# A cross-attention, state-space and expert block on one core: six of sixteen states added by DMA instead of TensorE, and token numbers scattered instead of rows

## The reference

```
x = x + cross_attention(norm(x), ctx)      # 8 heads, softmax(q k^T / 8) v, projections with bias
x = x + selective_scan(norm(x))            # 1024 channels, 16 states
x = x + experts(norm(x))                   # 16 experts, 4 per token, 2 of 4 groups of experts allowed
```

## Time and profile before

| | us |
|---|---|
| median of 3 runs | 1340.01 (1334.44 to 1340.54) |
| the profiled execution | 1334.18 |
| its span | 1332.2 |
| TensorE busy | 1143.1 (86%) |
| VectorE busy | 881.5 (66%) |
| ACT busy | 621.5 (47%) |
| POOL busy | 134.0 (10%) |
| bytes moved | 266.27 MB |

### The profile page before, as it was taken

How to read it: one execution, slowest core, us unless ns; L and a number is a source line. 1 busy time by engine, 2 the same in 40 slices (tenths; PEclk the granted TensorE clock), 3 DMA queues, 4 the chain that set the end, 5 groups by cost and what they waited for, 6 DMA issues and landing times.

```text
span 1332.2 us, 13289 instructions
## 1 busy us (share of the span) xinstructions
PE 1143.1 (86%) x4276; PEld 729.0 (55%) x4276; DVE 881.5 (66%) x946; ACT 621.5 (47%) x1366; POOL 134.0 (10%) x113
## 2 busy tenths in 40 slices
PE   6988769789797899998889989629999999999992
PEld 4875646566564567675557757324444445444451
DVE  1311579666757999967799995877999974224312
ACT  4542665435355655537556635624455422222321
POOL 0010003201000043000007000030000000233002
PEclk9998889989998999999899999759999998999997
DMA  8375006998601145340035331068999984999994
GB/s 281 111 245 194 4 17 221 404 396 326 223 9 16 33 125 175 78 145 0 17 72 150 119 123 44 0 225 274 360 357 351 375 316 152 375 357 406 410 382 126
DMA packets 115188, 266.27 MB, mean 200 GB/s; under 512 B 11280, under 2 KB 44208, under 8 KB 115120
## 3 DMA queue, kind: packets, MB, share of 16 engines
q1 hardware_dynamic: 99248, 207.22, 45.1%
q0 software_dynamic: 15872, 58.20, 11.1%
HBM read 197.07 MB, written 68.32 MB: 199 GB/s over the span
## 4 chain that ended last, share of the span: by engine, by line
PE 46%; DVE 35%; DMA 8%; ACT 7%; issue 3%; POOL 1%; SPq 0%; POOLq 0%; DVEq 0%; ACTq 0%
DVE state L1348 12%; PE bank L815 9%; PE bank L776 7%; DVE state L1345 6%; PE bank L683 5%; PE bank L695 4%; PE bank L836 4%; PE bank L716 4%; DVE decay L1352 3%; DMA ctx<-in_ctx_t 3%; DVE state L1355 3%; DVE y_acc L1359 2%; PE bank L632 2%; DMA bc_bcast<-bc_scratch 2%; PE bank L747 2%
## 5 line engine op out<-in xcount | busy, mean ns | idle before, releaser
L1348 DVE TENSOR_TENSOR_SCAN state<-decay,state 128x2048 f32<-128x2048 f32 x64 | 282.9, 4421 | 23.5 <-ACT decay L1102 22.6
L815 PE MATMUL bank<-expert_w,block_x_t 128*128 128x512 f32 x496 | 227.0, 601 | 1.8 <-ACT block_x_t L1154 1.7
L683 PE MATMUL bank<-decay,params 128*128 128x512 f32 x384 | 173.3, 595 | 5.9 <-DVE decay L1352 5.9
L1639 POOL DMA_INDIRECT dispatched<-ffn_x,slot x32 | 73.0, 2280 | 756.3 <-DVE slot L1441 747.7
L1102 ACT ACTIVATE decay<-delta_even,params 128x256 f32<-128x256 f32 x256 | 107.2, 498 | 82.7 <-PE bank L683 74.2
L815 PEld LDWEIGHTS bank<-expert_w,block_x_t 128*128 128x128 f32 x496 | 91.6, 195 | 93.7 <-issue 91.6
L695 PE MATMUL bank<-ctx,queries_ctx 128*128 128x256 f32 x512 | 125.6, 403 | 16.2 <-DMA ctx<-in_ctx_t 15.0
L716 PE MATMUL bank<-probs,ctx 128*128 128x256 f32 x512 | 121.2, 392 | 11.1 <-ACT probs L1009 6.4
L1102 ACT ACTIVATE decay<-delta_odd,params 128x256 f32<-128x256 f32 x256 | 106.2, 499 | 34.5 <-PE bank L683 24.9
L695 PEld LDWEIGHTS bank<-ctx,queries_ctx 128*128 128x128 f32 x512 | 102.1, 204 | 34.2 <-DMA ctx<-in_ctx_t 16.4
L1496 DVE SCALAR_TENSOR_TENSOR hidden<-hidden,bank 128x256 f32<-128x256 f32 x62 | 26.1, 421 | 142.7 <-ACT hidden L1158 141.7
(11 more groups left out here) (193 smaller groups left out, 1334.2 us busy)
## 6 DMA issues: line engine op xcount, KB each, us to landing
dispatched<-ffn_x POOLq DMA_DIRECT2D x38, 1024.0 KB, 27.2
expert_w<-in_eg_t SPq DMA_DIRECT2D x62, 512.0 KB, 6.4
expert_w<-in_eu_t SPq DMA_DIRECT2D x62, 512.0 KB, 9.6
expert_w<-in_ed_t SPq DMA_DIRECT2D x62, 512.0 KB, 9.6
ctx<-in_ctx_t SPq DMA_DIRECT2D x32, 512.0 KB, 7.5
ctx<-in_ctx_n SPq DMA_DIRECT2D x32, 512.0 KB, 4.1
bc_bcast<-bc_scratch SPq DMA_DIRECT2D x64, 256.0 KB, 5.8
block_x<-dispatched SPq DMA_DIRECT2D x62, 256.0 KB, 9.0
```

What stands on the lines that cost most here:

```text
L683: mm = pe.matmul(y_bank[c][:, :], ident, dA[(g * NS + j) % NDEC][:, c * 512:(c + 1) * 512], start=False, stop=(j == NS - 1))
L815: mm = pe.matmul(o, xbT[q % 2][:, c, :], w_gu[q % NW][:, :, c, :], start=(c == 0), stop=(c == DC - 1))
L1348: dve.tensor_tensor_scan(h, dA[n % NDEC][:, 0:sw], h, 0.0, ALU.mult, ALU.add).then_inc(scan_rd, 1)
L1639: pool.indirect_dma_start(xd[WAVE_OF[c]], bass.IndirectOffsetOnAxis(slot[:, i:i + 1].bitcast(U32), 0), fx[:, t, :], None).then_inc(dispatc ...
```

## The change

1. Of the 16 states of groups 0 to 2, six (0, 2, 4, 6, 8, 10) are added by DMA: POOL issues a transfer from the state's product in SBUF into `sum_s` in SBUF that adds to what is there. Each waits for the state's step and for the transfer before it. `sum_s` lies over `nrm_` (the normed `x`); ACT writes the `D` term into it (`y_start`, which now waits for `bc_out`), and TensorE adds it to the ten other states by the identity (`add_dma_sum`) just before states 12 and 13. `start_sum` goes. VectorE's `norm` waits until that was read. A decay buffer of a state added by DMA comes free when its transfer has landed.
2. ACT's decays in the preparation and in the units come one state later in its order (state s + 1 in the unit that scans s, where it was s + 2), and states 13 and 14 before the end of the attention.
3. The normed rows are stored once per group, in token order (`store_rows`); `dispatch` scatters 4-byte token numbers to the slots, for groups 0 and 1 in three parts between the adding transfers. The tables to clear hold numbers: two small transfers at the start.
4. SP loads a block's 128 token numbers six blocks ahead (`load_block_tokens`), and POOL gathers its rows by them (`gather_block`), three ahead, with the storing and collecting worked into the same queue.

```diff
+NID = 2 * NX
+BY_DMA = range(0, NS - TAIL - PRE, 2)
+BY_PE = [j for j in range(NS) if j not in BY_DMA]
+        sum_s = [nrm_[:, 0:NBK * GTS[g]] for g in range(NGR)]
...
# SP
-                if q >= NX:
-                    sp.wait_ge(xt_full, q - NX + 1)
-                sp.dma_start(xb[q % NX], xd[w][bass.DynSlice(row, P)]).then_inc(xb_in[q % NX], 16)
+                if q >= NID:
+                    sp.wait_ge(xb_in[q % NX], 16 * (q // NX - 1))
+                sp.dma_start(bid[:, q % NID:q % NID + 1], ids[w][bass.DynSlice(row, P)]).then_inc(bid_in[q % NID], 16)
...
-                    for j in range(NW):
+                    load_gate_up(w, 0)
+                    load_down(w, 0)
+                    for j in range(NID):
+                        load_block_tokens(w, j)
+                    for j in range(1, NW):
                         load_gate_up(w, j)
                         load_down(w, j)
-                    for j in range(NX):
-                        load_block_x(w, j)
...
# TensorE
-                if g > 0:
-                    start_sum(g - 1)
...
+            def add_dma_sum(g):
+
+                pe.wait_ge(sum_in, 16 * len(BY_DMA) * (g + 1))
                 for c in range(NBK * GTS[g] // 512):
+                    mm = pe.matmul(y_bank[c][:, :], ident, sum_s[g][:, c * 512:(c + 1) * 512], start=False, stop=False)
+                mm.then_inc(sum_read, 1)
...
+                if j in BY_DMA:
+                    return
...
                 if g > 0:
+                    add_dma_sum(g - 1)
                     for s in range(NS - TAIL - PRE, NS - PRE):
                         sum_state(g - 1, s)
...
# ACT
-                lead = list(range(2, LEAD + 2)) if g > 0 else []
+                lead = list(range(2, LEAD + 1)) if g > 0 else []
...
+                act.wait_ge(bc_out, 16 * (g + 1))
+                o = (sum_s if g in SUMMED else acc_s)[g]
...
+                elif j in BY_DMA:
+                    act.wait_ge(sum_in, 16 * (last * len(BY_DMA) + BY_DMA.index(j) + 1))
...
-                    now = [s + 2 for s in unit_states(g - 1, k)] if g > 0 else []
+                    now = [s + 1 for s in unit_states(g - 1, k)] if g > 0 else []
...
-                scan_decay(g, NS - TAIL)
+                for s in range(NS - TAIL - PRE + 1, NS - TAIL + 1):
+                    scan_decay(g, s)
...
# VectorE, in norm
+                if g:
+                    dve.wait_ge(sum_read, g)
...
# POOL
-            for i, (w, first, end) in enumerate(CLEARS):
-                n = CLEAR_UNITS[i * len(CLEAR_UNITS) // len(CLEARS)]
-                pool.wait_ge(s_full, n)
-                v = xd[w][first:end].rearrange("(p r) d -> p r d", p=P)
-                pool.dma_start(v, fx_[:, 0:D].unsqueeze(1).to_broadcast([P, (end - first) // P, D])).then_inc(cleared, 16)
+            for w in range(len(WAVES)):
+                n = ROWS[w] // P
+                pool.dma_start(ids[w].rearrange("(p r) o -> p (r o)", p=P), fx_[:, 0:n].bitcast(I32)).then_inc(cleared, 16)
...
+            def store_rows(c):
+
+                pool.wait_ge(fx_rdy, c + 1)
+                w = WAVE_OF[c]
+                first = (TILE0[c] - WTILES[w][0]) * P
+                rows = fxd[w][first:first + NTS[c] * P].rearrange("(t p) d -> p t d", p=P)
+                pool.dma_start(rows, fx[:, 0:NTS[c], :]).then_inc(fx_out, 16)
+
+            def add_state(g, i, j):
+
+                n = g * len(BY_DMA) + i
+                if i == 0:
+                    pool.wait_ge(ys_rdy, g + 1)
+                pool.wait_ge(step_done, g * NS + j + 1)
+                if n:
+                    pool.wait_ge(sum_in, 16 * n)
+                pool.dma_start(sum_s[g], dA[(g * NS + j) % NDEC][:, 0:NBK * GTS[g]], accum_op=ALU.add).then_inc(sum_in, 16)
+
+            def dispatch(c, part=0, parts=1):
...
+                    pool.indirect_dma_start(ids[WAVE_OF[c]], bass.IndirectOffsetOnAxis(slot[:, i:i + 1].bitcast(U32), 0),
+                                            token[:, t:t + 1], None).then_inc(dispatched, 16)
+
+            def gather_block(w, j):
+
+                q = BLOCK0[w] + j
+                if j == 0:
+                    pool.wait_ge(fx_out, 16 * (WAVES[w][-1] + 1))
+                pool.wait_ge(bid_in[q % NID], 16 * (q // NID + 1))
+                if q >= NX:
+                    pool.wait_ge(xt_full, q - NX + 1)
+                pool.indirect_dma_start(xb[q % NX], None, fxd[w],
+                                        bass.IndirectOffsetOnAxis(bid[:, q % NID:q % NID + 1].bitcast(U32), 0))\
+                    .then_inc(xb_in[q % NX], 16)
...
+            for g in SUMMED:
+                if g:
+                    store_rows(g - 1)
+                for i, j in enumerate(BY_DMA):
+                    add_state(g, i, j)
+                    if g and j > LEAD:
+                        dispatch(g - 1, i - 3, len(BY_DMA) - 3)
+            store_rows(NGR - 2)
+            dispatch(NGR - 2)
+            for j in range(BLOCKS[0]):
+                gather_block(0, j)
+                if j == OUT_STEP + 3 + NX:
+                    store_rows(NGR - 1)
+            dispatch(NGR - 1)
+            for j in range(BLOCKS[1]):
+                gather_block(1, j)
+                if j - NX == 2:
+                    blocks_written(0)
+                for i, t in enumerate(WTILES[0]):
+                    if j - NX == max(2 * i + 1, i + 2):
+                        collect(i, 0, t)
```

More of the change, by code:

```diff
@@ L194, in perceiver_block @@
         cnt = sb("expert_tokens", E)
+        token = sb("token", NTILES, I32)
+        bid = sb("block_token", NID, I32)
         iota = sb("iota_f32", 1 + JMAX + E * len(WAVES))
@@ L303, in perceiver_block @@
         yg_in = [sem(f"y_top_in{s}") for s in range(2)]
+        bid_in = [sem(f"block_token_in{s}") for s in range(NID)]
+        fx_out = sem("ffn_rows_written")
         dispatched = sem("tokens_dispatched")
@@ L342, in perceiver_block @@
         zero_rdy = sem("zero_rows_ready")
-        cleared = sem("dispatch_rows_cleared")
+        cleared = sem("slot_tokens_cleared")
+        tok_rdy = sem("token_numbers_ready")
         cst_rdy = sem("index_constants_ready")
@@ L541, in _ @@
                     if w == 0 and j == n - 2:
-                        for i in range(NX):
-                            load_block_x(1, i)
+                        for i in range(NID):
+                            load_block_tokens(1, i)
                     if w == 0:
@@ L1625, in _ @@
             pool.wait_ge(zero_rdy, 1)
-            for i, (w, first, end) in enumerate(CLEARS):
-                n = CLEAR_UNITS[i * len(CLEAR_UNITS) // len(CLEARS)]
-                pool.wait_ge(s_full, n)
-                v = xd[w][first:end].rearrange("(p r) d -> p r d", p=P)
-                pool.dma_start(v, fx_[:, 0:D].unsqueeze(1).to_broadcast([P, (end - first) // P, D])).then_inc(cleared, 16)
-            pool.wait_ge(cleared, 16 * len(CLEARS))
-            def dispatch(c):
-                pool.wait_ge(slot_rdy, c + 1)
-                for t in range(NTS[c]):
-                    for k in range(TOPK):
-                        i = (TILE0[c] + t) * TOPK + k
-                        pool.indirect_dma_start(xd[WAVE_OF[c]], bass.IndirectOffsetOnAxis(slot[:, i:i + 1].bitcast(U32), 0),
-                                                fx[:, t, :], None).then_inc(dispatched, 16)
+            for w in range(len(WAVES)):
+                n = ROWS[w] // P
+                pool.dma_start(ids[w].rearrange("(p r) o -> p (r o)", p=P), fx_[:, 0:n].bitcast(I32)).then_inc(cleared, 16)
@@ new lines, in _ @@
+            pool.wait_ge(cleared, 16 * len(WAVES))
+            pool.wait_ge(tok_rdy, len(WAVES))
+            def store_rows(c):
[12 more added lines that the diff above has]
+                pool.dma_start(sum_s[g], dA[(g * NS + j) % NDEC][:, 0:NBK * GTS[g]], accum_op=ALU.add).then_inc(sum_in, 16)
@@ new lines, in dispatch @@
+            def dispatch(c, part=0, parts=1):
+                pool.wait_ge(slot_rdy, c + 1)
+                picks = [(TILE0[c] + t, k) for t in range(NTS[c]) for k in range(TOPK)]
+                for t, k in picks[part * len(picks) // parts:(part + 1) * len(picks) // parts]:
+                    i = t * TOPK + k
+                    pool.indirect_dma_start(ids[WAVE_OF[c]], bass.IndirectOffsetOnAxis(slot[:, i:i + 1].bitcast(U32), 0),
+                                            token[:, t:t + 1], None).then_inc(dispatched, 16)
@@ L1650, in collect, with blocks_written @@
                         .then_inc(yg_in[n % 2], 16)
-            for c in range(NGR):
-                dispatch(c)
-            for w in range(len(WAVES)):
-                end = BLOCK0[w] + BLOCKS[w]
+            def blocks_written(w):
                 pool.wait_ge(yslot_rdy, w + 1)
                 for s in range(NX):
-                    pool.wait_ge(yb_out[s], 16 * len(range(s, end, NX)))
-                for i, t in enumerate(WTILES[w]):
```

(7 more changed lines are left out.)

30 lines of the change are left out of this document (14 added, 16 removed).

## The result

The changed kernel took 1353.25 us (median of 17 runs, 1342.03 to 1363.08), the one before, beside it, 1336.52 us (17 runs): ratio 1.0133, 95% interval 1.0104 to 1.0161. The ratio leaves out one run in a slower state of the chip (1363.08 us), so it isn't quite the quotient of the medians. The change makes the kernel slower by some 17 us, where I forecast 1311 us. The profiled execution took 1351.24 us, its span 1349.4.

The account below looks back on a forecast made before the run. No single limit: VectorE bound wave 0's experts beside group 3's scan, TensorE a stretch of wave 1. Terms -32.15 - 10.9 + 10.3 + 0 + 1.5 + 3 + 2 = -26.2 us gave 1308.0, forecast 1311 us, range 1298 to 1325.

Parts of the forecast that it names:

- The adding transfers, cost 0: In the units of a group's attention: each 1 MB add lands after about 10 us, so ACT's wait costs 0.
- cover (17 us): In the units: an add may take 17 us to land before ACT's wait for the decay buffer makes VectorE late.
- Rival B: In the units: adds crowd as the clears did, delaying `bc_bcast`; 18 adds at 1 us each, 1329 us; chance 0.13.
- Small packets cost little: In the block loop: 11 ns per packet, 160 per block costing each DMA engine 0.11 us.
- scattered numbers land sooner: At the start of wave 0: scatters carry 512 B in place of 256 KB, landing in about 2.5 us.
- Start of wave 0, +1.5: Ahead of wave 0: scatter, token load and gather take 11.3 us against 10.3; +1.5 us (-3 to +6).
- Wave 0 to wave 1, +3: At the change of waves: a gather behind a late token load adds issue and landing; +3 us (0 to +9).
- The clears, -32.15: In group 1: without clears of the dispatch rows it runs as group 2 does; -32.15 us.
- no gain from TensorE's fewer matmuls: In groups' units: 62 us of TensorE work goes, almost none on the path; taken as 0 (+3 to -6).
- the start of the sum: Eight matmuls leave their place ahead of routing logits or key projections: 3.63 us per group, -10.9; moved later, +10.3 us.
- the block loop inside a wave: Gathers replace loads of the same bytes three blocks ahead; small packets cost +2 us in wave 1 (0 to +5).
- Groups 2 and 3 moving by more than 3 us: Sign of a wrong forecast: would mean TensorE's load there was on the path after all.

Follow-up runs that it names:

- the square: Groups 2 and 3 together in four kernels: 512 B scatters 442.6 us without adds, 447.3 with; 4 B scatters 448.8 without, 472.1 with.

## Why the prediction was wrong

*The adding transfers, cost 0: the step that failed first.* Landing (9.1 us for 10) and cover (17 us) were right, and I asked only who waits for the sum. The landing was partly luck: the 7.6 us of the earlier trace rows that I called lone are of a load in the first microseconds, beside others, and say nothing of a transfer within SBUF. The cost lies with who shares the moment: 32.5 us between the medians, 29.8 between the profiled spans. Of these 8.1 us stand in group 1, which has no scatters, and 23.3 in groups 2 and 3; by the square 4.7 of the 23.3 are the adds' own and 18.6 their meeting with 4-byte scatters. Rival B named one of the two places, the late `bc_bcast` (24.3 us of waits in the whole kernel after), and priced the adds at 1 us each where they came to 1.8 (32.5 / 18); I gave it 0.13. The other place, the context load behind it, stood in no rival.

*"Small packets cost little", "scattered numbers land sooner": the step that failed second.* The 11 ns of the earlier trace rows are from a stretch whose one issue is a load, and I carried them to writes, for which no row stood; I wrote that myself and still gave the scatter a gain. The rule I weighed there (the Trainium skill, DMA: Bandwidth & Descriptors, Specifications: below 512 B a read-modify-write) fits the scatters: 12.5 us to land at 4 B, 5.7 at 512 B, and the weights beside them 12 to 17 us against 5 to 7. No run shows that a read-modify-write is the reason. The slow scatter should have been a rival with its own chance.

*Start of wave 0, +1.5:* from L1323 to the first transpose it was 57.9 us before, 62.7 after, and 56.8 to 57.0 in the three kernels whose scatters are all wide. So all 4.8 us are the narrow scatter's.

*Wave 0 to wave 1, +3:* it was 10.8. One part is SP's queue: POOL had issued the last scatter at 1143.2 us, but SP the first token load at 1168.49, behind wave 0's last weights and stores, and POOL the gather at 1177.15. The other part is the scatters, which slowed the weights.

*The clears, -32.15:* right for group 1, which without adds came within 0.5 us of the forecast. The start's 6.5 us, where five more clears stood, I had overlooked.

*Right:* no gain from TensorE's fewer matmuls; in group 1 the start of the sum (VectorE's decay wait 6.85 to 3.43 us, for 3.63; in group 2 its route wait gave back only 2.4 of 3.63, 7.07 to 4.67); the block loop inside a wave (+0.7 and +3.0 for +2). Groups 2 and 3 moving by more than 3 us, which I had called a sign of error, showed it, but not the meaning that I gave it: TensorE's load was not on the path.

The parts add up. The span came out 43.4 us above the forecast: the adds 31.4 in the groups, 12.8 behind group 3, 5.4 in groups 2 and 3 even without adds (448.8 us; wide scatters give back 6.2), 0.5 in group 1, less the start's 6.5 make 43.6.

## What to carry to other kernels

A transfer that lands in time can still cost: list what else its releasing event starts, and what stands behind those in their queues. Here one load put ahead of its neighbour in SP's queue gave back 14.6 us. Don't scatter 4-byte items beside other traffic: a row of 512 B of which one word counts was twice as quick to land. But clear its table where the DMA engines have room. Don't take the price of small writes from small loads.

## What the runs showed of the hardware

In this kernel's traffic an accumulating 1 MB transfer within SBUF landed after 9.1 us (median of 18), a plain one after 6.5. 20,224 words written 512 B apart cost 22.4 us beside the first weight loads, and 6.5 us when spread over a stage whose DMA share was 0.29 without them. And two disturbances of the DMA engines didn't simply add: they cost groups 2 and 3 4.7 and 6.2 us alone, 29.5 together.
